# Row maxima turned by VectorE and carried to their rows by four small transfers per unit

## Chip, cores and metric

One core of one Trainium2 chip runs the program once. The metric is the device time of one execution in microseconds, the median of several runs. Everything computed is float32; the matmuls that matter here read float32r operands.

## What is computed

The reference is a transformer block over x of shape 8 x 512 x 512: attention with 16 heads of 32 (a latent of 128 for keys, values and queries, and a rotary part shared by the heads), then a shared feed-forward layer and 16 routed experts, each behind a layer norm and a residual. The part that the change touches is the softmax:

```python
k = jnp.concatenate([k_c, k_rb], axis=-1)
q = jnp.concatenate([q_c, q_rb], axis=-1)
scores = jnp.einsum('bhsd,bhtd->bhst', q, k) / math.sqrt(HEAD_DIM)
attn = jax.nn.softmax(scores, axis=-1)
ctx = jnp.einsum('bhst,bhtd->bhsd', attn, v_c)
```

The maximum over t of each row s is subtracted before the exponential. The kernel does that with an extra operand row of the scores matmul.

## The kernel before

All five engines run one long list of steps, `K.order`, and each engine takes from it the steps that it has a function for (the dictionaries `stages`). Attention is cut into 32 units `u`: eight batches (`b = u // 4`) of four groups of four heads (`g = u % 4`). `beside_order` (L170) lays 16 scores steps of unit u over 32 slots and puts the work of other stages between them, at slots given in the table `STEP` (L153): the maxima of the next unit (`tops`), the step `rows` that brings them to their place, the values, the keys and queries of unit u + 2 (`half`, then `send`), and a share of the work of the neighbouring batches.

The steps that bear on the change, for unit u, all of them but the scores done while unit u - 1 is at work:

- `top(u, j, i)`, 16 of them (j a head of the group, i a block of 128 query rows): TensorE makes the scores with the queries on the partitions (L632), VectorE takes the maximum of each row into `K.mx` (L925), a number per query row.
- `rows(u)`: TensorE turns the maxima of four heads by four small transposes (L638) into one of the two banks `MS`, so that they lie along four partitions, head by head. ScalarE writes them times -1 into the rows 64 to 67 of `K.QR[:, u % 2, :]` (L1433).
- `scores(u, i, j)`: TensorE makes the scores with the keys on the partitions, in two matmuls into one bank: 128 rows of content parts (L646), and 68 rows (L651), of which the rows 64 to 67 multiply the negated maxima with a constant (`c_sel`, one at the head's own row). The first L651 of a unit waits until `rows(u)` is done. ScalarE takes the exponential (L1443), GpSimd adds the blocks up for the sum (L1637).
- `send(u)`: SyncE issues eight transfers of 256 KB from SBUF to SBUF that stack the operands of unit u (L1792 to L1799); the first `top(u)` and the scores wait for them.

SyncE issues nearly all other transfers as well, on one queue, in the order of the list: loads of x (L1765), the second copy of a batch (`again`, L1808), `qr` (L1782, L1783: the shared rotary part of the queries into `K.QR`), the stores of x1 (L1813), of h (L1818) and of the turned h (L1824), 1 MB each. They come once per batch: the load of x and the store of h while the unit with g = 2 is at work, the store of the turned h in g = 3, `again` at the start of g = 0, the store of x1 in g = 1.

The banks `MS` are filled by turns, in the order in which the steps named in `FILLS` (L361) stand in the list; whoever fills one waits until the filling before the last was emptied.

## Time and profile before

| what | us |
|---|---|
| median of 3 runs (1570.11 to 1578.66) | 1576.51 |
| span of the profiled execution | 1566.3 |
| TensorE busy in it (matmuls) | 1498.5 |
| VectorE busy | 974.3 |
| GpSimd busy | 803.9 |
| ScalarE busy | 783.3 |
| DMA queue of SyncE, share of the 16 engines | 58.0% |

The span runs from the first to the last instruction of the program; the time of the profiled execution itself, with what lies around the span, is not given apart, so the runs' median stands in its place, 10.2 us above the span. A busy TensorE is not one at its peak, since its matmuls overlap. The attention part lies between about 60 and 860 us; the feed-forward part follows.

### The profile page before, as it was taken

What the parts mean: (1) busy time and instruction counts of PE and PEld (TensorE: products, weight loads), DVE (VectorE), ACT (ScalarE), POOL (GpSimd) and SP (SyncE); (2) the same over time, 40 slices, a digit from 0 to 9 for tenths busy, and PEclk for the clock granted to TensorE, in tenths of its full rate; (3) what the DMA queues carried; (4) which work ended last, traced back from release to release, by engine and by line L of the source; (5) the groups of instructions that cost most, each with busy time, mean ns of one, the idle gap of its engine ahead of it and who ended that gap; (6) DMA issues with size and microseconds to landing.
All of it is one profiled execution on the core that took longest, in us unless ns stands there. A gap on an engine that the chain in (4) does not pass through costs nothing.

```text
span 1566.3 us, 21725 instructions
## 1 busy us (share of the span) xinstructions
PE 1498.5 (96%) x7006; PEld 1018.5 (65%) x7006; DVE 974.3 (62%) x1841; ACT 783.3 (50%) x1415; POOL 803.9 (51%) x812
## 2 busy tenths in 40 slices
PE   5699999999999999999998999999999999999998
PEld 3355666656656666566564578778666666668886
DVE  3657676767676767767667454862333333349988
ACT  3265567566565675665647455422222222275554
POOL 1076787787776977877859630003222222143341
PEclk9699999999999999999999999999999999999999
DMA  5878669589495795884956421536987777697773
GB/s 130 138 100 135 101 109 213 74 173 172 82 179 111 121 211 74 181 156 85 222 97 129 135 79 67 198 121 196 311 235 219 210 215 221 195 349 241 232 241 125
DMA packets 163926, 257.75 MB, mean 165 GB/s; under 512 B 20100, under 2 KB 70404, under 8 KB 161764
## 3 DMA queue, kind: packets, MB, share of 16 engines
q1 hardware_dynamic: 144584, 204.98, 58.0%
q0 software_dynamic: 12784, 41.82, 9.4%
q10 hardware_dynamic: 6448, 9.57, 1.8%
q8 instruction: 58, 0.95, 0.3%
q14 instruction: 52, 0.43, 0.1%
HBM read 103.74 MB, written 58.46 MB: 104 GB/s over the span
## 4 chain that ended last, share of the span: by engine, by line
PE 71%; DMA 10%; DVE 7%; POOL 4%; issue 3%; ACT 2%; SPq 2%; DVEq 0%; POOLq 0%; ACTq 0%
PE bank L113 12%; PE bank L724 9%; PE bank L792 8%; PE bank L815 8%; PE bank L646 6%; PE bank L632 6%; DMA a<-a 6%; PE bank L662 6%; PE bank L651 6%; PE bank L746 5%; POOL a L1637 2%; PE bank L671 2%; DMA f<-f 1%; SPq L1875 1%; PE bank L804 1%
## 5 line engine op out<-in xcount | busy, mean ns | idle before, releaser
L1637 POOL TENSOR_TENSOR a<-a 128x512 f32<-128x512 f32 x384 | 499.5, 1329 | 100.2 <-ACT a L1443 54.5
L1443 ACT ACTIVATE a<-bank 128x512 f32<-128x512 f32 x512 | 296.4, 597 | 258.4 <-PE bank L651 218.4
L925 DVE TENSOR_REDUCE a<-bank 128x1 f32<-128x512 f32 x512 | 321.3, 680 | 80.2 <-PE bank L632 79.7
L113 PE MATMUL bank<-a 128*128 128x512 f32 (+1 forms) x864 | 238.9, 398 | 2.7 <-DVE s L877 1.6
L646 PE MATMUL bank<-a 128*128 128x512 f32 x512 | 217.3, 424 | 5.0 <-ACT a L1443 4.9
L651 PE MATMUL bank<-a 68*128 68x512 f32 x512 | 203.8, 398 | 0.4 <-ACT a L1433 0.2
L632 PE MATMUL bank<-a 128*128 128x512 f32 x512 | 181.0, 425 | 22.7 <-DMA a<-a 17.8
L113 PEld LDWEIGHTS bank<-a 128*128 128x128 f32 (+1 forms) x864 | 158.9, 186 | 49.1 <-issue 6.7
L1701 POOL DMA_INDIRECT f<-h_scratch,f x79 | 75.4, 954 | 224.5 <-DMA f<-f 203.6
L746 PE MATMUL bank<-c 128*128 128x512 f32 x768 | 178.2, 391 | 4.2 <-DVE c L983 2.1
L724 PE MATMUL bank<-c 128*128 128x512 f32 x768 | 177.4, 390 | 1.3 <-ACT c L1484 1.3
L746 PEld LDWEIGHTS bank<-c 128*128 128x128 f32 x768 | 143.6, 188 | 36.1 <-DVE c L983 3.4
L724 PEld LDWEIGHTS bank<-c 128*128 128x128 f32 x768 | 143.7, 188 | 34.5 <-issue 3.8
L646 PEld LDWEIGHTS bank<-a 128*128 128x128 f32 x512 | 96.8, 189 | 99.5 <-ACT a L1443 52.0
L792 PEld LDWEIGHTS bank<-f 128*128 128x128 f32 x632 | 119.7, 190 | 52.4 <-issue 40.1
L792 PE MATMUL bank<-f 128*128 x632 | 149.6, 380 | 2.3 <-issue 1.5
L815 PE MATMUL bank<-f 128*128 x316 | 148.5, 593 | 0.0
L632 PEld LDWEIGHTS bank<-a 128*128 128x128 f32 x512 | 96.7, 194 | 75.9 <-DVE a L925 28.6
L1258 DVE TENSOR_TENSOR f<-f 128x256 f32<-128x256 f32 x79 | 33.4, 423 | 173.4 <-ACT f L1556 173.3
L662 PE MATMUL bank<-a 128*32 128x512 f32 x1024 | 134.6, 612 | 0.0
L651 PEld LDWEIGHTS bank<-a 68*128 68x128 f32 x512 | 97.0, 189 | 16.0 <-ACT a L1433 1.2
L1566 ACT COPY f<-bank 128x512 f32<-128x512 f32 x79 | 46.3, 586 | 120.5 <-PE bank L815 118.1
(190 smaller groups left out, 1766.9 us busy)
## 6 DMA issues: line engine op xcount, KB each, us to landing
a<-a SPq DMA_DIRECT2D x272, 256.0 KB, 9.7
f<-f SPq DMA_DIRECT2D x316, 64.0 KB, 3.9
yp_scratch<-f SPq DMA_DIRECT2D x79, 256.0 KB, 3.4
a<-in_L_attn_x SPq DMA_DIRECT2D x15, 1024.0 KB, 11.7
x_scratch<-a SPq DMA_DIRECT2D x8, 1024.0 KB, 4.6
h_scratch<-a SPq DMA_DIRECT2D x8, 1024.0 KB, 13.3
hT_scratch<-s SPq DMA_DIRECT2D x8, 1024.0 KB, 9.8
c<-hT_scratch SPq DMA_DIRECT2D x8, 1024.0 KB, 7.0
```

The costliest lines, as they stand in the source:

```text
L113: t = e.matmul(out, a[n], b[n], start=n == 0 and m == 0, stop=n == len(ah) - 1 and m == 2)
L632: e.matmul(MX[n % 3][:], K.Qc[z][:, j, i * P:(i + 1) * P], K.Kc[z][:, j, :], start=True, stop=True).then_inc(Z.top, 1)
L646: e.matmul(SC[n % 2][:], K.Kc[z][:, j, i * P:(i + 1) * P], K.Qc[z][:, j, :], start=True, stop=False)
L651: e.matmul(SC[n % 2][:], K.KR[0:68, b % 2, j, i * P:(i + 1) * P], K.QR[0:68, u % 2, :], start=False, stop=True).then_inc(Z.score, 1)
L662: t = e.matmul(CT[HD * j:HD * j + HD, :], K.v[:, u % VS, i, HD * j:HD * j + HD], K.pt[:, n % NP, :], start=i == 0, stop=i == 3)
L724: t = e.matmul(bank[:], (K.sul if a else K.suh)[:, k, cut], (K.hTl if c else K.hTh)[:, k, :], start=m == 0, stop=m == 11)
L746: t = e.matmul(bank[:], (K.aTl if a else K.aTh)[:, k, cut], (K.sdl if c else K.sdh)[:, k, :], start=m == 0, stop=m == 23)
L792: t = e.matmul(K.UP[z][:, 0:FI], K.hTt[:, z, k * P:(k + 1) * P], K.flat[:, bass.ds(reg[i] + k * FI, FI)], start=k == 0, stop=k == 3)
L815: t = e.matmul(K.DN[z][:], K.eaT[:, z, k * P:(k + 1) * P], K.flat[:, bass.ds(reg[i] + 4 * FI + k * D, D)], start=k == 0, stop=k == 1)
L925: e.tensor_reduce(K.mx[:, i, j:j + 1], K.MX[n % 3][:], AX.X, ALU.max).then_inc(Z.max, 1)
L1443: e.activation(K.pt[:, n % NP, :], K.SC[n % 2][:], ACT.Exp, scale=SCALE).then_inc(Z.exp, 1)
L1637: e.tensor_tensor(K.acc[:, j, :], a, K.pt[:, n % NP, :], ALU.add).then_inc(Z.acc, 1)
```

## The change

The maxima now go into the columns 4j + i of a 128 x 32 tile `K.mx`, of which the other 16 columns are zero. `rows(u)` becomes a step of VectorE and of SyncE. VectorE turns the tile in its 32 x 32 blocks (one instruction) into `K.mxt`: partition 32a + 4j + i then holds the maxima of head j for the 32 query rows 128i + 32a and on. SyncE issues four transfers, one for each a, from 16 partitions of 128 bytes each into the rows 64 to 67 of `K.QR`. TensorE's four transposes and ScalarE's negation are gone, and so is this filling of `MS`, which shifts which of the two banks later steps use. The minus sign moves into the constant `c_sel`. The step `rows` is put at an earlier slot of the unit, right behind the last `top`.

```diff
@@ STEP: one of the four entries
-        "divide0": 1, "round0": 15, "low0": 15, "k0": 3, "q0": 5, "rows0": 25, "values0": (16, 16, 29),
+        "divide0": 1, "round0": 15, "low0": 15, "k0": 3, "q0": 5, "rows0": 23, "values0": (16, 16, 29),
...
-FILLS = ("turn", "proj", "half", "rows", "v", "total", "project", "turn2", "route", "fold", "bias")
+FILLS = ("turn", "proj", "half", "v", "total", "project", "turn2", "route", "fold", "bias")
...
-    K.mx = tile([P, 4, 4])
+    K.mx = tile([P, HD])
+    K.mxt = tile([P, HD])
@@ TensorE
-    def rows(u):
-        bank = begin("rows", u)
-        w.wait_ge(Z.max, 16 * (u + 1))
-        for i in range(4):
-            t = e.transpose(bank[0:4, i * P:(i + 1) * P], K.mx[:, i, :], K.ident[:])
-        t.then_inc(*end("rows", u))
...
         e.matmul(SC[n % 2][:], K.Kc[z][:, j, i * P:(i + 1) * P], K.Qc[z][:, j, :], start=True, stop=False)
-        drained("rows", u)
+        w.wait_ge(Z.shift, 4 * 16 * (u + 1))
@@ VectorE
+    e.memset(K.mx, 0.0).then_inc(Z.turned, 1)
...
         w.wait_ge(Z.top, n + 1)
+        w.wait_ge(Z.turned, u + 1)
+        e.tensor_reduce(K.mx[:, 4 * j + i:4 * j + i + 1], K.MX[n % 3][:], AX.X, ALU.max).then_inc(Z.max, 1)
+
+    def rows(u):
+        w.wait_ge(Z.max, 16 * (u + 1))
         if u:
-            m = K.fill["rows", u - 1]
-            w.wait_ge(Z.full[m % 2], m // 2 + 1)
-        e.tensor_reduce(K.mx[:, i, j:j + 1], K.MX[n % 3][:], AX.X, ALU.max).then_inc(Z.max, 1)
+            w.wait_ge(Z.shift, 4 * 16 * u)
+        e.transpose(K.mxt, K.mx).then_inc(Z.turned, 1)
@@ ScalarE
-    def rows(u):
-        b = u // NG
-        bank = begin("rows", u)
-        if u >= 2:
-            w.wait_ge(Z.score, 16 * (u - 1))
-        e.mul(K.QR[64:68, u % 2, :], bank[0:4, :], -1.0).then_inc(*end("rows", u))
@@ SyncE
+    def rows(u):
+        w.wait_ge(Z.turned, u + 2)
+        if u >= 2:
+            w.wait_ge(Z.score, 16 * (u - 1))
+        shift = raw(K.QR[64:68, u % 2, :]).rearrange("j (i s) -> j i s", s=P)
+        for a in range(4):
+            e.dma_start(shift[:, :, a * HD:(a + 1) * HD], K.mxt[a * HD:a * HD + 16, :]).then_inc(Z.shift, 16)
@@ constants
-        "c_sel": np.ascontiguousarray(np.broadcast_to(np.eye(4, dtype=np.float32)[:, :, None], (4, 4, S))),
+        "c_sel": np.ascontiguousarray(np.broadcast_to(-np.eye(4, dtype=np.float32)[:, :, None], (4, 4, S))),
```

The queue of SyncE from a unit with g = 2 into the next with g = 3. Before (L1799: last transfer of a send; L1775, L1776: rotary part of the keys; L1765: load of x; L1818: store of h; L1782, L1783: `qr`; L1792: next send):

```order
L1799 DMA a<-a 32x4x512
L1775 DMA a<-a 32x4x512
L1776 DMA a<-a 32x4x512
L1765 DMA a<-in_L_attn_x 128x4x512
L1818 DMA h_scratch<-a 128x4x512
L1782 DMA a<-a 32x512
L1783 DMA a<-a 32x512
L1792 DMA a<-a 32x4x512 x3
```

And now (the lines are those of the changed kernel: L1758 the load of x, L1819 the store of h, L1784 the four new transfers, L1775 and L1776 `qr`):

```order
L1800 DMA a<-a 32x4x512
L1768 DMA a<-a 32x4x512
L1769 DMA a<-a 32x4x512
L1758 DMA a<-in_L_attn_x 128x4x512
L1819 DMA h_scratch<-a 128x4x512
L1784 DMA a<-a 4x4x32 x4
L1775 DMA a<-a 32x512
L1776 DMA a<-a 32x512
L1793 DMA a<-a 32x4x512 x3
```

The four new transfers stand between the store of h and `qr`; the rest keeps its order.

The queue of VectorE at the same place, before (L925: maxima, L905: rotary part, L942: low part of the context):

```order
L905 TENSOR_TENSOR a<-a 64x512
L925 TENSOR_REDUCE a<-bank 128x1 x9
L942 TENSOR_TENSOR a<-s,a 128x512
L925 TENSOR_REDUCE a<-bank 128x1 x3
L912 SCALAR_TENSOR_TENSOR a<-bank,a 128x512
```

And now (L919: maxima, L925: the turn of the 32 x 32 blocks):

```order
L901 TENSOR_TENSOR a<-a 64x512
L919 TENSOR_REDUCE a<-bank 128x1 x9
L925 STREAM_TRANSPOSE a<-a 128x32
L942 TENSOR_TENSOR a<-s,a 128x512
L919 TENSOR_REDUCE a<-bank 128x1 x3
```

The turn comes right behind the last maximum of the unit, ahead of the low part of the context. On TensorE the four transposes L638 are taken out of the end of the unit, and no other matmul moves.

## Rows read from the trace of the kernel before

**Rows 1.** The page, head and part 1: busy us, share, instructions of each engine.

```profile
span 1566.3 us, 21725 instructions
...
PE 1498.5 (96%) x7006; PEld 1018.5 (65%) x7006; DVE 974.3 (62%) x1841; ACT 783.3 (50%) x1415; POOL 803.9 (51%) x812
```

**Rows 2.** Windows, one unit, columns: stretch, length, busy of PE, PEld, DVE, ACT, POOL, clock, DMA.

```profile
448.90:473.70 24.80, 24.80 (x143) 16.18 (x142) 16.25 (x31) 17.89 (x32) 18.50 (x21) 1.00 1.02 237
```

**Rows 3.** Timeline at the end of unit 14: start, length, engine, line, operation, idle before.

```profile
445.01 0.59 SPq L1818 DMA_DIRECT2D h_scratch<-a  x1
...
445.54 0.69 DVE L925 TENSOR_REDUCE a<-bank 128x1 f32<-128x512 f32 x1 [1.16 <-PE bank L632]
...
448.89 0.56 SPq L1782 DMA_DIRECT2D a<-a  x1
...
448.93 0.40 PE L651 MATMUL bank<-a 68*128 68x512 f32 x1
```

**Rows 4.** DMA view, issues of 445.01, 448.89, 449.50, 464.14, 517.03; last column us to landing.

```profile
h_scratch<-a SPq DMA_DIRECT2D x1, 1024.0 KB, 13.9
...
a<-a SPq DMA_DIRECT2D x1, 64.0 KB, 9.2
...
a<-a SPq DMA_DIRECT2D x1, 64.0 KB, 10.7
...
hT_scratch<-s SPq DMA_DIRECT2D x1, 1024.0 KB, 10.6
...
a<-a SPq DMA_DIRECT2D x1, 256.0 KB, 12.1
```

**Rows 5.** Chain of waits around 446.7 us: start, length, engine, line.

```profile
446.75 0.44 PE bank L638 x4
```

**Rows 6.** L1433 (ACT, negation), durations min/median/max in ns.

```profile
L1433 ACT ACTIVATE a<-bank x32: 585/586/588, 59.9 to 856.9; 4x512 fp32r<-4x512 f32 x32
```

**Rows 7.** VectorE, groups of 60 to 860 us.

```profile
L934 DVE RECIPROCAL a<-a 128x16 f32<-128x16 f32 x30 | 7.6, 254 | 1.0
```

**Rows 8.** The page, DMA issues, the smallest near an empty queue.

```profile
out<-c SPq DMA_DIRECT2D x1, 128.0 KB, 2.0
```

**Rows 9.** Line views of L1818, then of L1765: landing.

```profile
DMA to landing us min/median/max: 4.3/13.3/14.4
...
DMA to landing us min/median/max: 12.1/12.5/14.9
```

**Rows 10.** Timeline at other unit ends: last maximum, store or first score.

```profile
133.66 1.38 SPq L1765 DMA_DIRECT2D a<-in_L_attn_x  x1
...
139.32 0.39 PE L651 MATMUL bank<-a 68*128 68x512 f32 x1
...
473.75 0.40 PE L651 MATMUL bank<-a 68*128 68x512 f32 x1
...
492.34 0.69 DVE L925 TENSOR_REDUCE a<-bank 128x1 f32<-128x512 f32 x1 [0.48 <-PE bank L632]
...
502.30 0.40 PE L651 MATMUL bank<-a 68*128 68x512 f32 x1
...
529.16 0.40 PE L651 MATMUL bank<-a 68*128 68x512 f32 x1
...
854.86 0.67 DVE L925 TENSOR_REDUCE a<-bank 128x1 f32<-128x512 f32 x1
...
857.91 0.40 PE L651 MATMUL bank<-a 68*128 68x512 f32 x1
```

**Rows 11.** Windows around the first long stall.

```profile
43.80:48.20 4.40, 0.06 (x2) 0.01 (x1) 2.98 (x2) 1.90 (x1) 0.00 (x0) 0.81 1.05 187
61.30:69.90 8.60, 0.01 (x1) 0.00 (x0) 0.04 (x1) 0.60 (x1) 2.46 (x8) 0.50 0.85 118
69.90:73.80 3.90, 3.88 (x9) 3.11 (x10) 2.58 (x4) 1.30 (x2) 0.00 (x0) 0.50 0.00 0
73.90:78.00 4.10, 3.77 (x17) 2.76 (x16) 2.65 (x5) 3.12 (x6) 0.52 (x1) 1.00 0.29 62
```

More of the change, by code:

```diff
@@ L383, in __init__ @@
         self.top, self.max = make("top_full"), make("max_done")
+        self.turned, self.shift = make("mx_turned"), make("shift_in")
         self.score, self.exp, self.acc, self.pv = make("score_full"), make("exp_done"), make("acc_done"), make("pv_done")
@@ L817, in e_down @@
         t.then_inc(Z.ed, 1)
-    stages = {"turn": turn, "proj": proj, "v": v, "half": half, "bias": bias, "top": top, "rows": rows, "scores": scores,
+    stages = {"turn": turn, "proj": proj, "v": v, "half": half, "bias": bias, "top": top, "scores": scores,
               "values": values, "total": total, "project": project, "turn2": turn2, "route": route, "fold": fold, "up": up,
@@ L1342, in finish @@
         e.tensor_tensor(K.x1[:, z, :], K.x1[:, z, :], K.sh[:, z, :], ALU.add).then_inc(Z.co, 1)
-    stages = {"stat": stat, "aggr": aggr, "sel": sel, "split w": split_w, "turn": turn, "low": low, "proj": proj, "half": half, "bias": bias, "top": top, "invert": invert,
+    stages = {"stat": stat, "aggr": aggr, "sel": sel, "split w": split_w, "turn": turn, "low": low, "proj": proj, "half": half, "bias": bias, "top": top, "rows": rows, "invert": invert,
               "project": project, "fold": fold, "split h": split_h, "split up": split_up, "split down": split_down, "up": up,
@@ L1601, in finish @@
                      scale=K.crw[:, z, 4, 0:1]).then_inc(Z.cn, 1)
-    stages = {"split w": split_w, "round": round_, "scale": scale, "turn": turn, "proj": proj, "v": v, "half": half, "rows": rows, "scores": scores, "keep": keep,
+    stages = {"split w": split_w, "round": round_, "scale": scale, "turn": turn, "proj": proj, "v": v, "half": half, "scores": scores, "keep": keep,
               "turn2": turn2, "route": route, "split h": split_h, "split up": split_up, "round up": round_up,
@@ L1936, in finish @@
         e.dma_start(K.outv[t][:, cut], K.x1[:, z, cut]).then_inc(Z.cs[z], 16)
-    stages = {"load": load, "proj": proj, "qr": qr, "send": send, "again": again, "residual": residual, "scale": scale, "turn2": turn2, "early su": early_su,
+    stages = {"load": load, "proj": proj, "qr": qr, "rows": rows, "send": send, "again": again, "residual": residual, "scale": scale, "turn2": turn2, "early su": early_su,
               "early hT": early_hT, "load sd": load_sd, "split h": split_h, "weights": weights, "prepare": prepare, "move": move, "e down": e_down,
```

6 rows, old and new, of the table STEP are left out of this document.

## The prediction, made before the changed kernel ran

> **What bounds the kernel now.** I read the page first: TensorE is busy for 1498.5 us of the 1566.3 us span [rows 1]. The attention part (about 60 to 860 us, 32 units of work, four to a batch) was then cut into units with the windows view. In the unit that starts at 448.90 us TensorE is busy for all 24.80 us at the full granted clock, while VectorE, ScalarE and GpSimd have 16 to 19 us of work each, so anything that stops TensorE lengthens the kernel [rows 2]. The same row shows the DMA engines as full as TensorE (share 1.02). So the next view is the timeline at a unit's end [rows 3], to see how much time lies between the last row maximum of a unit (starts 445.54, ends 446.23) and the first scores matmul that needs the negated maxima (L651, 448.93): 2.70 us. And the DMA view tells what the sync queue holds at that moment [rows 3, 4]. A 1 MB store to h_scratch is issued at 445.01 and lands 13.9 us later, at 458.9. The two 64 KB transfers issued behind it, at 448.89 and 449.50, land after 9.2 and 10.7 us, at 458.1 and 460.2. They are small, yet they come out where the store does: **transfers of this queue leave it in the order in which they were issued.**
>
> **The change, part by part.**
> TensorE loses four 4x128 turns per unit, 0.44 us on the chain of waits [rows 5]. 32 units x 0.44 = 14.1 us, the whole gain that can be expected there. One filling of the two shared banks goes too; no wait of weight stands at it, so I cost it at nothing.
> ScalarE loses one negation per unit, 0.586 us x 32 = 18.8 us [rows 6]. It lies beside TensorE work; I take nothing for it. The minus sign moves into a constant and costs nothing.
> VectorE gains a turn of 128x32 per unit. The trace has no such shape; its nearest row is the 128x16 reciprocal with 0.25 us [rows 7], the lower bound is nothing. I take 0.2 us: 6 us in 32 units on an engine with a third of its time free. It counts only as part of the delay below.
> Sync gains four transfers of 2 KB per unit. Behind the waiting instruction on that queue stand, at most, the store of x1, the reload of x and the next unit's sends, which start over 5 us into a unit: no one waits for those. Who waits for the four is TensorE, at the first scores of a unit.
>
> So the cost is the landing of the four against that first matmul, which without the turns starts 0.44 us earlier. **The four have a time of their own**: turn and semaphores 0.3 us, three issues of 0.6 us before the last (0.56 us each for a 64 KB one [rows 3]), and 2.0 us to land, the fastest landing of the trace [rows 8]: about 4.2 us after the last maximum. And they have **the queue's time**: not before what was issued ahead of them, plus 0.3 us. The later one counts. Unit by unit (g is the unit's place in its batch):
>
> Into g=3, batches 1 to 6: the h store stands ahead. In the case of 448.93: 458.9 + 0.3 = 459.2 against 448.5, a wait of 10.7 us. The median store lands after 13.3 us instead of 13.9 [rows 9], so I take 10.1 us, times 6 = 61 us. In batch 0 the load of x stands there: issued 133.66, landing 12.1 us later at 145.8, plus 0.3, against 139.32 - 0.44: 7.2 us [rows 9, 10]. In batch 7 the store lands early, so the own time decides: last maximum 855.53 + 4.2 = 859.7 against 857.5, 2.2 us [rows 9, 10]. Sum 70 us.
> Into g=0 (seven): hT store, issued 464.14, lands 474.7, plus 0.3, against 473.75 - 0.44: 1.7 us [rows 4, 10]. But after the long wait the unit before starts on an empty queue, so this store should land some 0.6 us sooner in relation: 1.1 x 7 = 8 us.
> Into g=2 (eight): the sends of the next unit are ahead, the last issued 517.03, landing 529.1, plus 0.5, against 529.16 - 0.44: 0.9 x 8 = 7 us [rows 4, 10].
> Into g=1: last maximum 493.03 + 4.2 = 497.2 against 502.30 - 0.44: no wait [rows 10]. For the first two units, where TensorE already stood for transfers (8.60 us in a row with 0.01 busy), I add 1 us each [rows 11].
> Waits together: 70 + 8 + 7 + 2 = 87 us.
>
> **The clock.** After the 8.60 us without work the granted clock was 0.50 (1.2 GHz) and stayed there for the next 3.90 us of work, with 9 matmuls, against 17 in the 4.10 us after it at 1.00 (2.4 GHz); an idle stretch of 4.40 us already saw it fall (mean 0.81) [rows 11]. So 3.9 us at half rate lose about 1.9 us. The seven waits of 7 to 11 us each are long enough: 7 x 1.9 = 13 us. The Trainium skill (TensorE: Matmul & The Clock Gate, The HAM clock gate) says the same of an engine left idle; the trace agrees, and the sum uses the trace alone.
>
> Sum: 87 + 13 - 14 = +86 us. While TensorE stands, ScalarE and GpSimd work off what they are behind; TensorE's short waits for them are few, so I take 3 us back: **+83 us**. Against the profiled span that is 1566.3 + 83 = 1649.3 us. The span leaves out 10.2 us to the median of the runs shown (1576.5), in which the start and end around it lie; the profiled execution's own time isn't given apart. Forecast: 1576.5 + 83 = **1660 us**.
>
> **One rule of the skill against the rows.** The rows 3 and 4 show small transfers held by the store ahead. The Trainium skill (DMA: Bandwidth & Descriptors, Anatomy of one DMA) gives a transfer about 2.0 us fixed plus its bytes over a rate, that is some 2 us for 2 KB, with no word of what is ahead of it; by that price alone the sum would be that of the first rival. The same page (Queues, rings and completion order) has descriptors consumed in ring order on each engine, which the trace bears out, and splits a transfer over the largest number of rings, up to 16, that divides both outer sizes: 4 here, for 4 and 16. By that the four need only four of sixteen rings to be clear, which changes neither term as long as all rings are equally full.
>
> **The rivals.**
> 1. The small transfers pass what is queued, and only their own time counts (not slower). For it: they are tiny, and touch few of the engines. Against it: the two transfers behind the store [rows 3, 4]. Waits: into g=3 4.2 - 2.26 = 1.9 x 8 = 16 us, into g=0 0.4 x 7 = 3, start 1, less 14: +6 us. With issues of half that length (three of them 0.9 us less in all) it is -1 to -4. It decides where the four land within 2.3 us of the last maximum. Time: 1572 to 1583, say 1576; 7 in 100.
> 2. The order holds, but the waits are shorter: the store's data has left the rings some us before its write to memory is confirmed, or TensorE makes up time in the unit after. For it: the transfer of 448.89 lands 0.8 us before the store. Against: that is all of the difference, and the next one lands 1.3 us after. If a third of each long wait goes and no clock is lost in half of them: 83 - 23 - 7 = +53, 1630 us; 12 in 100.
> 3. The clock stays down for most of the unit after each long wait, since the unit begins with waits of its own. For it: nothing after 73.9 us. Against: 17 matmuls in 4.1 us at 1.00 right after the recovery. Its price goes to a unit of 24.80 us with 143 matmuls at half the rate, less what lies under waits: up to 15 us more x 7 = 105; half of that: +135, 1711 us; 4 in 100.
>
> **How the numbers follow.** My forecast's case has 77 in 100. Its own range comes from the long waits' landing (9.0 to 11.5 us each, +-9 us over seven), the short waits (8 to 25 us), the clock (0 to 25 us) and what is made up (0 to 15): 1635 to 1690. The range of 8 in 10 reaches into the second rival: 1622 to 1695. About 0.5% (8 us) is what a measurement of this kernel can tell from no change. Faster needs rival 1 with every saving: 0.02; within 0.5%: 0.05, the rest of rival 1; slower: 0.93.
>
> **What would show it.** In the changed profile TensorE should have gaps of 7 to 11 us before the first score's second matmul of seven units, spaced one batch apart, released by the small transfers, whose issue stands right after the h store and whose landing comes at or just after that store's. Each gap should be followed by some 4 us at a granted clock of 0.5. The units into g=1 should have no gap. The forecast is wrong if the four transfers land 2 to 3 us after issue while the store is still out, if the gaps are there but the next unit is shorter by as much, or if no gap shows and the span is near 1566 us.

## The result, and the profile after

| | us |
|---|---|
| before, median of 4 runs (1570.11 to 1578.66) | 1577.45 |
| changed, median of 4 runs (1664.62 to 1668.37) | 1666.47 |
| ratio, with its 95% interval | 1.0564 [1.0543, 1.0585] |

The changed kernel is slower by 89 us. The forecast was 1660 us, +83. The ratios here and below are over undisturbed runs; in e6, e7 and e12 they differ from the ratio of the two medians by 0.2 to 0.45%.

The head and part 1 of the changed kernel's page, then the line of its part 5 in which the difference stands:

```profile
span 1662.8 us, 21650 instructions
...
PE 1508.8 (91%) x6878; PEld 1025.6 (62%) x6878; DVE 979.5 (59%) x1874; ACT 769.4 (46%) x1383; POOL 801.2 (48%) x812
...
L646 PE MATMUL bank<-a 68*128 68x512 f32 x512 | 212.5, 415 | 92.4 <-DMA a<-a 92.4
```

TensorE was busy for 96% of the span [rows 1] and is now for 91%, with 128 fewer matmuls and yet 10 us more of busy time: part of its work ran at the lower clock, as the sums below show. One wait holds nearly all of the difference: the scores matmul with the maxima (L651 before, L646 now) stood for transfers for 92.4 us. Which transfers, the view of the one line that issues the four tells (count, time of one issue in ns, first and last start, then who waited):

```profile
L1784 SPq DMA_DIRECT2D a<-a x128: 625/632/713, 58.0 to 941.9; - x128
...
  PE bank L646: 92.4, 25
```

The timeline at the end of unit 14, the same place as [rows 3] (start, length, engine, line, operation; in brackets the idle time before it and who ended it), with the DMA view's landing time of the store ahead of the four; those of the 2 KB transfers are not recorded:

```profile
476.37 0.36 SPq L1819 DMA_DIRECT2D h_scratch<-a  x1
476.93 0.69 DVE L919 TENSOR_REDUCE a<-bank 128x1 f32<-128x512 f32 x1 [1.16 <-PE bank L634]
477.65 0.21 DVE L925 STREAM_TRANSPOSE a<-a 128x32 f32<-128x32 f32 x1
477.89 2.73 SPq L1784 DMA_DIRECT2D a<-a  x4
...
490.17 0.79 PE L646 MATMUL bank<-a 68*128 68x512 f32 x1 [10.18 <-DMA a<-a]
```

```profile
h_scratch<-a SPq DMA_DIRECT2D x1, 1024.0 KB, 13.0
```

The four are issued by 480.6, and the wait ends at 490.17. The store ahead of them, issued at 476.37, lands 13.0 us later, at 489.4. The matmul follows 0.8 us behind. The same row of other units (into g=3 of batch 0, into g=0 of batch 4, into g=3 of batch 6, and the last two units):

```profile
146.62 0.79 PE L646 MATMUL bank<-a 68*128 68x512 f32 x1 [7.53 <-DMA a<-a]
517.38 0.50 PE L646 MATMUL bank<-a 68*128 68x512 f32 x1 [0.32 <-DMA a<-a]
834.82 0.80 PE L646 MATMUL bank<-a 68*128 68x512 f32 x1 [7.75 <-DMA a<-a]
918.87 0.79 PE L646 MATMUL bank<-a 68*128 68x512 f32 x1 [3.09 <-DMA a<-a]
943.58 0.80 PE L646 MATMUL bank<-a 68*128 68x512 f32 x1 [3.18 <-DMA a<-a]
```

A matmul that begins a unit starts 0.23 us behind the one before it when nothing holds it. Measured against that (start less start, less 0.23), the 32 waits come to 97.4 us; the same sum is 1.7 us before. Into g=3: 7.7, then 10.4, 10.45, 10.3, 10.3, 10.5, 7.9 and, in batch 7, 3.4. Into g=0 0.45 to 1.5, into g=2 0.4 to 1.1 and once 3.25, into g=1 none but 0.3 in the first. The rest, 11.8 us (0.8 before), is the wait of the very first unit, which cost nothing: in the kernel before, TensorE stood for 8.60 us soon behind that place [rows 11], and the scores of unit 1 start at 92.7 us there and at 91.7 now.

The clock (windows view: stretch, length, busy time and count of PE, PEld, DVE, ACT, POOL, granted clock, DMA share and rate), in the wait of unit 15 and behind it:

```profile
480.30:490.17 9.87, 0.00 (x1) 0.01 (x1) 0.00 (x0) 0.09 (x1) 3.40 (x3) 0.73 0.93 284
490.20:495.10 4.90, 4.90 (x16) 4.14 (x17) 1.89 (x3) 2.04 (x4) 0.00 (x0) 0.50 0.00 0
495.10:499.10 4.00, 4.00 (x21) 2.19 (x20) 2.10 (x4) 2.81 (x5) 0.00 (x0) 0.99 0.00 1
```

It falls to 1.2 GHz while TensorE stands (a mean of 0.73 over the wait) and stays there for the first 4.9 us of work, in which 16 matmuls fit, against 21 in the 4.0 us behind it. It also falls where the wait was short. Two more windows, behind the wait of 1.1 us into g=0 that ends at 286.69 and behind that of 3.25 us that ends at 918.87:

```profile
286.90:290.30 3.40, 3.40 (x9) 2.65 (x9) 2.11 (x4) 1.19 (x2) 3.36 (x3) 0.50 0.89 304
...
918.80:925.20 6.40, 6.33 (x17) 4.33 (x21) 4.39 (x7) 2.68 (x5) 5.91 (x10) 0.50 0.92 315
```

**How far the attention part has moved.** The last scores matmul starts at 881.5 us before and at 967.4 now (first and last start are in each line's view):

```profile
L651 PE MATMUL bank<-a x512: 389/395/792, 60.5 to 881.5; 68*128 68x512 f32 x171
```

```profile
L646 PE MATMUL bank<-a x512: 389/395/797, 68.7 to 967.4; 68*128 68x512 f32 x171
```

So the part that the change touches is 85.9 us longer. From the scores of unit 1 on (92.7 before, 91.7 now) to that last start I took three sums from the trace: the length, the time in which no matmul runs, and the time in which one runs at a clock of 0.50, half of which is lost against full rate:

| | length | idle | at 0.50 | length - idle - half of that |
|---|---|---|---|---|
| before | 788.8 | 15.3 | 6.8 | 770.0 |
| changed | 875.7 | 92.0 | 54.1 | 756.6 |

The last column is TensorE's work at full rate, and 13.4 us less of it is left: the turns. In the twelve kernels below, which all do without the turns, it lies between 754.0 and 761.2 us, so the three columns account for their differences. Of the +86.9 us of length, 76.7 are idle, 23.6 the clock, and -13.4 the work.

The rest of the profiled span, which the change doesn't touch, is 10.6 us longer too (684.8 before, 695.4 now). TensorE stands in it for 25.5 us against 18.5, 6.2 us of that in one wait for ScalarE at 1504.8 us, and does 7.5 us of its work at a clock of 0.50 against none, which is worth 3.7. Over the fourteen profiles the rest lies between 684.8 and 698.9 us, shortest in the three in which TensorE does no work at 0.50 there. I compare kernels by their timed ratios, and the parts of a profile by the three sums.

### The profile page after: what moved, and what is told of

Its sections match the earlier page's. It is cut to its first block, busy times and chain, and to the rows that moved or that the text cites. A ratio compares the mean times of both kernels' runs of the same rounds, so it can differ in the third digit from the quotient of the medians.

```text
span 1662.8 us, 21650 instructions
## 1 busy us (share of the span) xinstructions
PE 1508.8 (91%) x6878; PEld 1025.6 (62%) x6878; DVE 979.5 (59%) x1874; ACT 769.4 (46%) x1383; POOL 801.2 (48%) x812
## 4 chain that ended last, share of the span: by engine, by line
PE 71%; DMA 9%; DVE 9%; SPq 3%; ACT 3%; issue 2%; POOL 2%; another core or an unknown queue 1%; DVEq 0%; POOLq 0%; ACTq 0%
PE bank L113 10%; PE bank L719 10%; PE bank L787 8%; DMA a<-a 8%; PE bank L810 8%; PE bank L741 7%; PE bank L634 6%; PE bank L646 6%; PE bank L641 5%; PE bank L657 5%; DVE a L919 4%; SPq L1784 3%; PE bank L666 2%; POOL a L1630 2%; PE bank L680 1%
## 5 line engine op out<-in xcount | busy, mean ns | idle before, releaser
L1630 POOL TENSOR_TENSOR a<-a 128x512 f32<-128x512 f32 x384 | 497.8, 1324 | 182.1 <-PE bank L666 124.9
L919 DVE TENSOR_REDUCE a<-bank 128x1 f32<-128x512 f32 x512 | 321.9, 681 | 159.6 <-PE bank L634 159.2
L646 PE MATMUL bank<-a 68*128 68x512 f32 x512 | 212.5, 415 | 92.4 <-DMA a<-a 92.4
L641 PE MATMUL bank<-a 128*128 128x512 f32 x512 | 220.5, 431 | 8.2 <-ACT a L1436 8.1
L634 PE MATMUL bank<-a 128*128 128x512 f32 x512 | 186.6, 437 | 8.3 <-DMA a<-a 4.5
L741 PE MATMUL bank<-c 128*128 128x512 f32 x768 | 180.1, 394 | 10.2 <-ACT c L1492 6.2
L646 PEld LDWEIGHTS bank<-a 68*128 68x128 f32 x512 | 100.3, 196 | 117.6 <-DMA a<-a 102.6
L641 PEld LDWEIGHTS bank<-a 128*128 128x128 f32 x512 | 99.1, 194 | 107.1 <-ACT a L1436 59.6
L634 PEld LDWEIGHTS bank<-a 128*128 128x128 f32 x512 | 101.4, 202 | 58.3 <-DVE a L919 27.6
```

The costliest lines, as they stand in the source:

```text
L634: e.matmul(MX[n % 3][:], K.Qc[z][:, j, i * P:(i + 1) * P], K.Kc[z][:, j, :], start=True, stop=True).then_inc(Z.top, 1)
L641: e.matmul(SC[n % 2][:], K.Kc[z][:, j, i * P:(i + 1) * P], K.Qc[z][:, j, :], start=True, stop=False)
L646: e.matmul(SC[n % 2][:], K.KR[0:68, b % 2, j, i * P:(i + 1) * P], K.QR[0:68, u % 2, :], start=False, stop=True).then_inc(Z.score, 1)
L741: t = e.matmul(bank[:], (K.aTl if a else K.aTh)[:, k, cut], (K.sdl if c else K.sdh)[:, k, :], start=m == 0, stop=m == 23)
L919: e.tensor_reduce(K.mx[:, 4 * j + i:4 * j + i + 1], K.MX[n % 3][:], AX.X, ALU.max).then_inc(Z.max, 1)
L1630: e.tensor_tensor(K.acc[:, j, :], a, K.pt[:, n % NP, :], ALU.add).then_inc(Z.acc, 1)
```

## The experiments

The theory was: the four transfers land when the queue ahead of them has landed; a wait of 10 us costs itself and a fall of the clock; and TensorE's turns are worth up to 14 us. The rivals: the four are slow in themselves, or the clock or the earlier slot of `rows` carries the loss. All expectations were written before the runs. Ratios are to the kernel before on the same chip; the last three columns are the profile's start of the last scores matmul, and TensorE's idle time and its work at 0.50 before it, as above (before: 881.5, 15.3, 6.8; changed: 967.4, 92.0, 54.1).

| run | edit to the changed kernel | us | ratio | last start | idle | at 0.50 |
|---|---|---|---|---|---|---|
| e1_store_behind | store of h behind the four | 1645.26 | 1.0431 [1.0398, 1.0464] | 956.5 | 75.4 | 63.6 |
| e2_both_behind | load of x behind them too | 1632.77 | 1.0359 [1.0324, 1.0394] | 935.7 | 59.3 | 52.9 |
| e3_act_queue | ScalarE issues the four | 1698.32 | 1.0766 [1.0730, 1.0802] | 1000.3 | 94.9 | 105.4 |
| e4_no_wait | nothing waits for the four | 1573.03 | 0.9975 [0.9961, 0.9989] | 876.1 | 20.9 | 12.4 |
| e5_all_vector | no transfer; turns and product on VectorE | 1576.41 | 0.9991 [0.9969, 1.0012] | 879.7 | 22.3 | 10.2 |
| e6_old_slots | `rows` at its slots of before | 1711.25 | 1.0874 [1.0833, 1.0914] | 1017.8 | 124.8 | 87.0 |
| e7_eight | eight transfers for four | 1720.54 | 1.0875 [1.0819, 1.0932] | 1020.6 | 124.9 | 91.0 |
| e8_one_turn | no transfer; one turn, four products | 1622.75 | 1.0335 [1.0318, 1.0351] | 936.2 | 55.0 | 59.4 |
| e9_act_no_wait | e4 with ScalarE issuing | 1653.73 | 1.0548 [1.0531, 1.0566] | 962.5 | 65.2 | 93.8 |
| e11_spread_late | wide turns, copy by ScalarE, old slots | 1608.07 | 1.0215 [1.0192, 1.0239] | 912.6 | 46.5 | 29.0 |
| e10_spread | the same, slots of the change | 1604.22 | 1.0184 [1.0151, 1.0217] | 907.1 | 37.4 | 36.6 |
| e12_spread_vector | the same, copy by VectorE | 1587.93 | 1.0076 [1.0045, 1.0106] | 913.6 | 43.0 | 35.8 |

One of the four runs of e7 took 6008.56 us, for a reason that I didn't find; the ratio leaves it out, and the other three took 1708.73 to 1721.28.

### What stands ahead in the queue (e1, e2)

```diff
@@ SyncE, e2; e1 holds back the store alone
+    held = []
     def load(b):
-        filled("proj", b - 1, "r")
-        e.dma_start(K.xt[:], x_d[b]).then_inc(Z.x, 16)
+        def fetch(): ...
+        if b > 1:
+            held.append(fetch)
+        else:
+            fetch()
...
             e.dma_start(shift[:, :, a * HD:(a + 1) * HD], K.mxt[a * HD:a * HD + 16, :]).then_inc(Z.shift, 16)
+        while held:
+            held.pop(0)()
...
         if i == 3 and kind == "h":
-            w.wait_ge(Z.scaled["h"], 4 * (b + 1))
-            e.dma_start(hv[b], K.yb[:]).then_inc(Z.h2s, 16)
+            def store(): ...
+            if b < B - 1:
+                held.append(store)
+            else:
+                store()
```

> The store of h is issued behind the four small transfers instead of ahead of them; nothing else moves. Theory (the transfers leave the sync queue in the order of issue): now the load of x is what stands ahead in batches 1 to 6. It landed 2.7 us before the store in the changed kernel (486.7 against 489.4), so the six waits into g=3 fall from 10.4 us to about 7.5, the clock still falls after them, and the time goes from 1666 to about 1648 (1643 to 1653). Rival (the small transfers are slow by themselves, as pieces of 128 bytes on four partitions, or the engines are full): the waits stay near 10 us and the time near 1666.

> The load of x and the store of h are both issued behind the four small transfers. Theory: what stands ahead is the rotary part of the keys, which landed at 484.2 against a first score at 479.8, so the waits into g=3 are some 4 to 5 us, in batch 0 too; 7 x 5.5 us less, and where the clock does not fall or comes back sooner up to 10 us more: 1618 to 1632, say 1626. Rival (slow by themselves): 1660 to 1670. A third outcome, that the late load of x holds up VectorE's next statistics, would show as waits of the maxima for the load of x and a time over 1640.

The timeline of e1 at the end of unit 14 (the store is L1824 here):

```profile
478.53 2.72 SPq L1786 DMA_DIRECT2D a<-a  x4
481.30 0.44 SPq L1824 DMA_DIRECT2D h_scratch<-a  x1
...
488.21 0.79 PE L646 MATMUL bank<-a 68*128 68x512 f32 x1 [7.56 <-DMA a<-a]
```

And of e2 (L1761 the load, L1829 the store):

```profile
468.95 2.71 SPq L1791 DMA_DIRECT2D a<-a  x4
471.70 0.44 SPq L1761 DMA_DIRECT2D a<-in_L_attn_x  x1
472.19 0.52 SPq L1829 DMA_DIRECT2D h_scratch<-a  x1
...
476.00 0.80 PE L646 MATMUL bank<-a 68*128 68x512 f32 x1 [4.93 <-DMA a<-a]
```

The waits into g=3 step down as the queue ahead is emptied: in batches 1 to 5, 10.3 to 10.5 us with load and store ahead, 7.7 to 8.0 with the load alone, 5.1 to 5.6 with neither. The time of e1 lies in what was expected; e2 missed by a little (waits of 4 to 5 us and 1618 to 1632 us expected, 1632.77 measured). The transfers are the same four, so they aren't slow in themselves; **what is ahead of them is**. At this place the matmul goes 0.7 to 0.8 us behind the landing of the last transfer ahead each time: of the store (489.4 and 490.17), in e1 of the load (487.46 and 488.21), in e2 of the rotary part of the keys (475.21 and 476.00). The idle time falls with them, 92.0, 75.4, 59.3 us. The clock gives nothing back (54.1, 63.6, 52.9 us at 0.50): it falls behind a wait of 5 us as behind one of 10.

### Another engine's queue (e3, e9)

```diff
@@ ScalarE, e3 and e9; rows is taken from SyncE
+    def rows(u):
+        w.wait_ge(Z.turned, u + 2)
...
+        for a in range(4):
+            e.dma_start(shift[:, :, a * HD:(a + 1) * HD], K.mxt[a * HD:a * HD + 16, :]).then_inc(Z.shift, 16)
```

> The same four transfers, issued by ScalarE on its own queue, with the wait for VectorE's turn on ScalarE. Theory (queue order): they pass the sync queue, and only their own time counts, 4 to 5 us after the last maximum: waits into g=3 of 2 to 3 us, the others near 0, 15 to 25 us in all instead of 97, and no fall of the clock. Against it stands ScalarE's time at four issues (some 0.63 us each, 2.5 us a unit in which no exponential runs), which TensorE feels in part: up to 60 us. Together 1580 to 1625, say 1600. Rival (the 16 engines are what is full, whatever the queue): the waits stay at 8 to 10 us and the time is over 1650.

This missed by far, and was the most telling run. The waits into g=3 of batches 0 to 6 fell to 3.9 to 4.8 us, yet the time rose. ScalarE at the end of unit 14, with the store of h that SyncE issued at 496.12, and TensorE (the order in the fence is SyncE, ScalarE, TensorE):

```profile
496.12 0.72 SPq L1819 DMA_DIRECT2D h_scratch<-a  x1
...
497.62 2.64 ACTq L1434 DMA_DIRECT2D a<-a  x4
500.31 1.09 ACT L1444 ACTIVATE a<-bank 128x512 f32<-128x512 f32 x2 [3.24 <-issue]
...
500.96 0.80 PE L641 MATMUL bank<-a 128*128 128x512 f32 x1 [2.10 <-ACT a L1444]
...
506.08 0.80 PE L646 MATMUL bank<-a 68*128 68x512 f32 x1 [3.47 <-DMA a<-a]
```

Two things stand in it. On their own queue the four do pass the store: it lands at 508.7 (12.6 us), and the matmul goes at 506.08. But their last one, issued at 499.62, still took about 6.5 us, not 2.0. Over these 6.5 us the sixteen DMA engines had a share of 1.06 (windows view), so they were full of the other queue's work. In the changed kernel, into the last unit, the same step took 1.7 us (last issue 941.86, matmul 943.58) with that share at 0.02. The Trainium skill (DMA: Bandwidth & Descriptors, Issuing engines are not separate DMA queues) says that transfers of different issuers run on the same engines and interleave, which these numbers bear out. And ScalarE pays: four issues of 0.64 to 0.66 us, in which its next exponential stands for 3.24 us and TensorE behind it for 2.10.

That page of the Trainium skill adds that another issuer saves only the time to initiate a transfer, "usually small relative to the DMA itself". To weigh this time alone I took the waiting away and left the issuing, on SyncE (e4) and on ScalarE (e9):

```diff
@@ e4, e9: TensorE waits for the zeroed rows only; the four go to rows nobody reads
-        w.wait_ge(Z.shift, 4 * 16 * (u + 1))
+        w.wait_ge(Z.rope0, 1)
...
-        shift = raw(K.QR[64:68, u % 2, :]).rearrange("j (i s) -> j i s", s=P)
+        shift = raw(K.QR[96:100, u % 2, :]).rearrange("j (i s) -> j i s", s=P)
```

> Leaves out the subtraction of the row maxima: the four transfers are issued as in the changed kernel, but into rows that nobody reads, TensorE does not wait for them, and the rows 64 to 67 hold zero. Everything else (maxima, turn, issues, slots) is as in the changed kernel. Theory: the whole loss is TensorE's wait for the landing and the clock after it, so the kernel ends up below the one before by the four turns of TensorE: 1577 - 14 = 1563, between 1558 and 1570. Rival (a share of the loss lies in the transfers or their issue, which delay the sends behind them, or in the other order of the banks): 1575 to 1600.

> The version without the wait (maxima not subtracted, transfers into rows that nobody reads), with the four transfers issued by ScalarE instead of SyncE. If ScalarE's time at the issues is what made the version on ScalarE's queue slow, its loss shows here without any wait for a landing: the first score of a unit came 2.6 us later after the last maximum there, 32 x 2.6 = 83 us on top of 1573, so 1640 to 1665. Rival (that version was slow through the landings alone): 1573 to 1585.

The waits of TensorE in e9, from 60 to 960 us (waited for: us in total, times, longest):

```profile
PE bank L642 <- ACT a L1446: 53.7, 42, 4.1
```

The issues cost nothing on SyncE (e4 is at 0.9975) and 5.5% on ScalarE, as much as 32 x 2.64 us, 84 us, of issuing, although ScalarE is busy for only half of the span. By the sums it comes in two parts: against e4 TensorE stands for 44 us more (65.2 against 20.9) and works 81 us more at the low clock (93.8 against 12.4), which is worth 41. The unit's exponentials come one by one and hand TensorE's two score banks back, so a hole of 2.6 us among them isn't hidden, and many of these stops (the clock falls 22 times between the second unit and the end of the attention part) are followed by a stretch at half rate. "Small relative to the DMA itself" is true here of 0.64 us against 6.5, and says nothing of the engine that issues.

e4 also prices the term of the sum that was taken for sure. It should have been 14 us faster than before, and was 4 (0.25%); its last start is 5.4 us earlier. The work at full rate is 12.4 us less (757.6 against 770.0), so the turns are gone nearly in full, but TensorE stands for 5.6 us more (in this stretch it waits for the sends for 7.9 us against 4.8, and for ScalarE for 7.0 against 4.3) and works 5.6 us more at 0.50. Part of a saving on the busiest engine turns into waits for the next slowest.

### The slot of rows (e6)

```diff
-"rows0": 23, ... "rows1": 21, ... "rows2": 25, ... "rows3": 25,
+"rows0": 25, ... "rows1": 26, ... "rows2": 28, ... "rows3": 28,
```

> The change with the step rows at the slots that it had before (25, 26, 28, 28 instead of 23, 21, 25, 25). Theory (the later of the own time and the queue's time decides): into g=3 the queue decides, so those waits stay at 10.4 us; into g=0 and g=2 the own time takes over, since the turn comes 2 to 3 us later, and those waits grow from about 0.9 and 0.5 us to about 2.5 and 1.1; into g=1 there is still room. Together some 17 us more: 1675 to 1690, say 1683. Rival (all waits are the queue's): 1666, as the change.

The timeline of e6 into a unit with g=2, and what the DMA view has for the store of x1 (L1814):

```profile
472.99 0.75 DVE L880 SCALAR_TENSOR_TENSOR a<-bank,a 128x512 fp32r<-128x512 f32 x1 [2.89 <-ACT a L1406]
473.65 0.20 DVE L925 STREAM_TRANSPOSE a<-a 128x32 f32<-128x32 f32 x1
...
475.28 0.36 SPq L1814 DMA_DIRECT2D x_scratch<-a  x1
475.69 3.37 SPq L1784 DMA_DIRECT2D a<-a  x4
...
480.25 0.79 PE L646 MATMUL bank<-a 68*128 68x512 f32 x1 [4.18 <-DMA a<-a]
```

```profile
x_scratch<-a SPq DMA_DIRECT2D x1, 1024.0 KB, 4.3
```

The waits into g=3 of batches 1 to 5 are as they were (10.3 to 10.6 us), as expected, since the same store is ahead either way. The miss is elsewhere: into g=2 of batches 1 to 6 the waits are 4.2 to 4.8 us, not 1.1, and those of batch 7 are 7.1 us into g=2 and 8.5 into g=3. The last maximum ended at 470.09, and the four are issued from 475.69. Of these 5.6 us 3.6 are VectorE's: its turn has come behind a step that waits for ScalarE, and starts at 473.65. Another 1.4 us are SyncE's: at slot 26 the four have come behind the store of x1 (slot 23), and SyncE waits for that store's data until 475.28. The idle time grows by 32.8 us, and the clock takes half of another 32.9. So the earlier slots are part of what keeps the change at +89 and not +134 (by the medians): what an order of steps costs includes **what stands ahead on each engine of the path, and what that waits for**.

### The number of transfers (e7)

> Twice the transfers: four of the same shape into rows that nobody reads are issued ahead of the four that count. Theory (own time against queue time): the last issue comes 2.8 us later, 7.9 us after the last maximum. Waits into g=3 in batches 0 to 6, where the queue decides, stay as they are within 0.5 us (10.4); into g=0 they go from 0.9 to about 4 us, into g=2 from 0.5 to about 2, into g=1 they stay at 0; about 40 us in all: 1695 to 1715, say 1706. Rival (each of these transfers of 128-byte pieces costs time on the rings): the waits into g=3 grow by 1 us or more as well, and the time is over 1720.

The edit puts four dead transfers of the same kind ahead of the four. The waits into g=3 grow by 0.8 us only (11.0 to 11.35 in batches 1 to 5), for four issues of 0.63 are 2.5 us and lie under the store's landing. That is between the 0.5 us of the theory and the 1 us of the rival; what the 0.8 us are was not tested. Those into g=0, where now the own time decides, grow from 0.5 to 1.5 us to 2.9 to 4.2. The windows view behind such a wait (the one that ends at 548.74):

```profile
548.70:553.00 4.30, 4.26 (x10) 3.39 (x11) 2.58 (x4) 1.19 (x2) 1.66 (x2) 0.50 0.73 244
```

10 matmuls in 4.3 us at 0.50, behind a wait of 3 us. The waits come to 133 us against 97 (about +40 was expected), the idle time to +32.9 us, and the work at 0.50 to +36.9, half of which, 18 us, is what the expectation had too little of.

### Without transfers (e5, e8)

```diff
@@ VectorE, e5
-        e.transpose(K.mxt, K.mx).then_inc(Z.turned, 1)
+        for a in range(4):
+            e.transpose(K.mxt[64:96, a * HD:(a + 1) * HD], K.mx[a * HD:(a + 1) * HD, :]).then_inc(Z.turned, 1)
+        w.wait_ge(Z.turned, 4 * u + 5)
...
+        e.tensor_tensor(K.QR[64:80, u % 2, :].rearrange("r (i s) -> r i s", s=P),
+                        K.mxt[64:80, :].unsqueeze(1).broadcast_to([16, 4, P]),
+                        K.mask[64:80, :].unsqueeze(2).broadcast_to([16, 4, P]), ALU.mult).then_inc(Z.shift, 1)
@@ VectorE, e8: the one turn stays, and four products, one from each quarter of the partitions
+            e.tensor_tensor(K.QR[64:80, u % 2, :].rearrange("r (i s) -> r i s", s=P)[:, :, at.start:at.start + HD],
+                            K.mxt[at, :].unsqueeze(1).broadcast_to([16, 4, HD]),
+                            K.mask[at, :].unsqueeze(2).broadcast_to([16, 4, HD]), ALU.mult).then_inc(Z.shift, 1)
```

VectorE's turn can write to other partitions than it reads, so four turns of 32 x 32 bring the maxima next to their rows. A product with a mask of minus ones keeps from each of 16 rows the part that is its own. The matmul then has 80 rows for 68, at the same 395 ns.

> A version without transfers: VectorE turns the maxima in four blocks of 32x32 straight into partitions 64 to 95, which gives 16 rows of 128 (one per head and block of rows), and one VectorE product with a mask of minus ones and zeros spreads them over 512 columns of the operand's rows 64 to 79; the constant has 16 rows and the second scores matmul reads 80 rows instead of 68. No turn on TensorE, no negation on ScalarE, no filling of a shared bank, no wait for a landing. Theory (the loss is the landing alone, and what can be had without it is what the kernel without the wait showed): no wait of the first score, about 1.3 us of VectorE work a unit in its place, 1570 to 1577, a hair below the kernel before. Rival (VectorE's extra 1.3 us a unit hold up the maxima, 32 x 1.3 = 42 us on an engine that TensorE waits for at the ends of units): 1585 to 1615.

> As the all-VectorE version, with less work in it: one turn of 128x32 in place of four of 32x32 (0.20 us each there), and four products of 16 partitions x 128 elements, which also shift the rows to partitions 64 to 79, in place of one of 512 elements (1.34 us there). Theory: the last product is done about 1.4 us after the last maximum instead of 2.2, so the 0.3 us that TensorE still waited into g=3 goes, and the kernel comes near the one without a carry (1573): 1571 to 1576. Rival (the four products cost as much as the one, each being held by something fixed): 1576 to 1580.

e5's turns and its product in the view of their lines (min/median/max in ns), and the one wait for it:

```profile
L927 DVE STREAM_TRANSPOSE a<-a x128: 202/203/208, 57.6 to 855.0; 32x32 f32<-32x32 f32 x128
```

```profile
L932 DVE TENSOR_TENSOR a<-a x32: 682/1382/1823, 58.5 to 855.3; 16x512 fp32r<-16x512 f32 x32
```

```profile
PE bank L647 <- DVE a L932: 3.8, 9, 2.2
```

e5 runs level with the kernel before and is the best version that computes everything. It shows that the loss lies in the transfers: the same maxima, turned by the same engine, cost nothing without them. e8 was to show the same with fewer instructions, and lost 3.4%. The view of its product, and its VectorE timeline at one place, with GpSimd's at the same time:

```profile
L933 DVE TENSOR_TENSOR a<-a x128: 282/1239/9861, 59.2 to 911.7; 16x128 fp32r<-16x128 f32 x128
```

```profile
549.07 10.81 DVE L933 TENSOR_TENSOR a<-a 16x128 fp32r<-16x128 f32 x4
```

```profile
548.89 1.29 POOL L1674 TENSOR_TENSOR a<-a 128x512 f32<-128x512 f32 x1
550.13 2.53 POOL L1640 TENSOR_TENSOR a<-a 128x512 f32<-128x512 f32 x2
552.62 1.28 POOL L1674 TENSOR_TENSOR a<-a 128x512 f32<-128x512 f32 x1
553.85 4.94 POOL L1640 TENSOR_TENSOR a<-a 128x512 f32<-128x512 f32 x4
```

Four products that take 0.28 us each at best last 10.81 us, 9.86 of them in the first, as long as GpSimd works without a pause. TensorE waited 34.4 us for them in all, and the clock fell with it. In e5 VectorE's product met such a row of GpSimd instructions too, and was through after 1.82 us, while GpSimd went on:

```profile
264.15 6.70 POOL L1639 TENSOR_TENSOR a<-a 128x512 f32<-128x512 f32 x5
264.16 1.82 DVE L932 TENSOR_TENSOR a<-a 16x512 fp32r<-16x512 f32 x1
```

### Which instructions wait for GpSimd (e11, e10, e12)

If products with two inputs are what waits, a kernel without any on this path should not. I put the maxima of block i into a tile of their own, so that four turns of 32 x 128 leave every row complete; one copy to `K.QR` is left, by ScalarE (times -1) or by VectorE (the sign in `c_sel`):

```diff
-    K.mx = tile([P, HD])
+    K.mx = tile([P, 4, HD])
...
+        spread = K.stage.rearrange("r (i s) -> r i s", s=P)
+        for a in range(4):
+            e.transpose(spread[:, :, a * HD:(a + 1) * HD], K.mx[a * HD:(a + 1) * HD, :, :]).then_inc(Z.turned, 1)
@@ ScalarE, e10 and e11; in e12 VectorE: e.tensor_copy(K.QR[64:80, u % 2, :], K.stage[0:16, :])
+        e.mul(K.QR[64:80, u % 2, :], K.stage[0:16, :], -1.0).then_inc(Z.shift, 1)
```

> A version without transfers and without VectorE products. The maxima are written into a tile of 128 x 4 x 32 that is zero but for column 4j + i in block i, so that four turns of VectorE (32 partitions x 128) give the 16 rows already spread over 512 columns; ScalarE copies them, times -1, into the operand (16 partitions x 512, as long as the negation before, 0.59 us). The step stands at the slots of the kernel before (25, 26, 28, 28). No TensorE turn, no shared bank. Theory (what the small products cost in the last version was a wait for GpSimd, which instructions with one input do not have): the turns take 0.2 to 0.35 us each whatever GpSimd does, no wait of TensorE of weight at the first score, ratio to before 0.995 to 1.000. Rival (VectorE's four more instructions or ScalarE's wait for them hold up TensorE): ratio over 1.003.

> The same with the step at the slots of the change (23, 21, 25, 25), right behind the last maximum. ScalarE then waits for the last maximum and the four turns, up to 2 us a unit in which no exponential runs. If waiting ScalarE is what delays TensorE (part of what made the version on ScalarE's queue slow), this one is slower than the other by 10 to 40 us; if only the issue of transfers on ScalarE was to blame there, both are equal within 4 us.

> As the last two, with the copy into the operand made by VectorE (one input, 16 x 512, 0.65 us by the nearest shape) instead of ScalarE, at the slots of the change, the minus sign in the constant. If ScalarE's waiting for VectorE was what cost those versions 2%, it is gone here: the operand is ready about 4 x 0.30 + 0.65 = 1.95 us after the last maximum, in time for every first score but perhaps 0.1 us into g=3; ratio to before 0.994 to 1.000. Rival (the turns on VectorE themselves hold up TensorE): ratio 1.01 or more.

The copy by ScalarE in e11 (part of the line view: busy us, mean ns, idle before it and whom it waited for), then the turns and the copy of e12:

```profile
L1434 ACT ACTIVATE a<-a 16x512 fp32r<-16x512 f32 x31 | 19.4, 626 | 41.4 <-DVE a L927 41.3
```

```profile
L927 DVE STREAM_TRANSPOSE a<-a x128: 302/303/307, 59.4 to 889.2; 32x128 f32<-32x128 f32 x128
```

```profile
L931 DVE CAST a<-a x32: 417/1038/8953, 60.8 to 889.6; 16x512 fp32r<-16x512 f32 x32
```

The turns never wait for GpSimd (302 to 307 ns in 128 of them), and VectorE's copy does, five times for 8.9 to 8.95 us, each time until 0.3 us after GpSimd's row of instructions ended, though it has one input. My guess of the two inputs was too narrow, and e11 and e12 missed. e10 and e11 lose to something else: ScalarE stands for the turns for 41.3 us in e11 and 49.8 in e10, and TensorE waits for its exponentials for 28.4 and 29.6 us, against 4.9 before and 8.0 in e12, where ScalarE has no part in the step. e10 was expected to lose 10 to 40 us against e11 if ScalarE's waiting were to blame. It was 4 us faster; but ScalarE waits for the turns in both, so the pair can't tell, and it is the comparison with e12 that speaks for the waiting. That e10 with the earlier slots is no slower also shows that the slot is not the reason. The runs of e12 scatter (1570.87 to 1600.59 us) and its profile is one of the longest (span 1598.8), so I take the durations from it; by its ratio it is 0.8% slower than the kernel before.

## Why the prediction was right, and where its terms were off

The forecast was +83 us, the measured difference is +89, and in the profiles the attention part grew by 85.9. By terms, in us:

| term | forecast | measured |
|---|---|---|
| waits into g=3, eight | 70 | 71.1 |
| into g=0, seven | 8 | 5.8 |
| into g=2, eight | 7 | 7.4 |
| into g=1, start of the part | 2 | -0.8 (0.3 less 1.1) |
| made up (less idle elsewhere) | -3 | -7.9 |
| clock | 13 | 23.6 |
| TensorE's turns | -14.1 | -13.4 |

The misses partly cancel (the clock took 10.6 us more, 4.9 more were made up, and the waits besides those into g=3 were 4.6 less), so that the total is nearer than its terms is in part luck.

- **The queue's time** was right. The waits into g=3 of batches 1 to 5 were 10.3 to 10.5 us against 10.1, batch 0's 7.7 against 7.2, and e1 and e2 show the cause by moving it. There the matmul went 0.7 to 0.8 us behind the store's landing, where 0.3 stood. Two entries inside were off and partly cancel: batch 6, whose store landed after 11.5 us and not 13, waited 7.9 us (and its matmul went 0.1 us before that landing, so the order isn't exact), and batch 7 3.4 where 2.2 stood. Those into g=2 were 0.4 to 1.1 us in seven of eight, and one, at the end of the attention part, 3.25. Into g=0 the store of the turned h decided, as forecast: it landed at 517.21, and the matmul went at 517.38.
- **The own time** of 4.2 us took the landing of 2.0 us from an empty queue [rows 8]. That was right where the engines were idle: 1.7 us from the last issue to the matmul into g=3 of batch 7, and 1.7 into g=0 of e7 (547.01 and 548.74). The issues were 0.67 to 0.73 us apart (0.6 taken), the turn took 0.21 us (0.2 taken). Under load the landing is longer: 6.5 us in e3, where no store was ahead on its own queue. What batch 7 waited above the forecast is the turn, which the forecast had right behind the last maximum. It stood behind a product of the feed-forward part and began 1.7 us late:

```profile
937.86 1.83 DVE L979 TENSOR_TENSOR c<-f,c 128x512 fp32r<-128x512 f32 x1
939.62 0.20 DVE L925 STREAM_TRANSPOSE a<-a 128x32 f32<-128x32 f32 x1
```

- **The clock** is the term that was mis-sized, 13 us for 23.6. Behind the seven long waits it was low for 3.1 to 6.0 us of work (32 us together, or 16 lost; the forecast had 3.9 each, from [rows 11]). The other 22 us lie in five stretches that the forecast didn't have, since it let only waits of 7 us and more bring the clock down: behind waits of 1.1, 1.4, 3.25 and 3.4 us, and one near the end, behind a stop of 2.1 us. Before there were two, each with 3.4 us of work, behind stops of 1.9 and 2.0 us; the second is at that same place near the end.
- **The turns** went nearly in full, 13.4 us of 14.1. As a gain in time they are worth less: in e4, where no wait for the four hides it, 4 us were left, since other waits and the clock took the rest.
- **ScalarE's and VectorE's terms** at nothing hold as far as e4 tells: it has both and is no slower than the kernel before. The same engines are not free for everything, though: issuing on ScalarE (e9) cost its full time.
- **The 10.2 us** between span and median were put down to what lies around the span. That was wrong: a run's time is 1.8 us above its span (1664.62 against 1662.8), and 1.8 or 1.9 us in all 64 runs of the kernel before that were timed beside the experiments. The profiled execution before was a fast one, at about 1568 us below all four runs of the first table. The clock is a part of that: its mean was 0.988 in the profile, 0.986 to 0.989 in those of the 64 with a span up to 1567.4 us, and 0.981 to 0.985 in those with 1575.0 and more. A difference of 0.003 over 1570 us is 4.7 us, by my estimate about half of what lies between them. What starts the fall stays open; no run was made for it.
- **The rivals.** That small transfers pass is refuted on the same queue (e1, e2) and true across queues (e3), where it doesn't help. The price of some 2 us that the prediction takes from the Trainium skill (DMA: Bandwidth & Descriptors, Anatomy of one DMA) is fitted there to transfers that GpSimd issues; here SyncE's took 1.7 us with the DMA engines idle, and what is queued comes on top. Shorter waits: not seen. The clock staying down for most of a unit: not seen, at most 6.0 us of work behind a long wait (and 21 matmuls in 4.0 us right behind 495.1), though right in that the clock would cost more than 13 us.

No version here that computes everything beats the kernel before; e5 equals it.

## What to carry to other kernels

A small transfer costs what is queued ahead of it, not its bytes: before putting one on a path with little slack (2.7 us here), add up what the queue holds at that moment and what its issuer still waits for. If the path is TensorE's, count the fall of the clock too, behind short waits as well: in these kernels each us of added idle time brought 0.3 to 0.9 us more (e4 and e5 aside, where both are small). Moving the issue to a compute engine's queue trades this for that engine's time, 2.64 us for four here, which a half-idle engine can't hide when it feeds TensorE one tile at a time. The sums of idle time, half of the work at low clock and the rest split any such difference into its causes.

## What the runs showed of the hardware, unexpected

- VectorE can be held across several instructions of GpSimd: up to 9.9 us for one 16x128 product (0.28 at best), up to 8.95 us for one 16x512 copy (0.42 at best), while the turns kept their time within 6 ns. The Trainium skill (SBUF — State Buffer, SBUF: two separate sides) has an exclusive lock between the two engines, held "for the whole instruction", against which VectorE's two-input work and its faster modes compete. That it is exclusive agrees; that the loser stands through eight instructions of the other in a row (548.89 to 558.79) is more than it says. It isn't always so: the product of e5, also with two inputs, took at most 1.8 us, though GpSimd's instructions followed each other as closely there. Why stays open.
- Transfers on ScalarE's queue passed a 1 MB store on SyncE's that was issued 1.5 us ahead, and still needed 6.5 us for 2 KB with the DMA engines full (share 1.06). With a share of 0.02 the same took 1.7 us.
- TensorE's clock fell to 1.2 GHz around waits of only 1.1 to 3.4 us, and was low for 3.4 to 6.4 us of the work behind them; most other waits of about 1 us had no fall. What makes the difference stays open.
- The matmul with 80 rows for 68 took the same time (medians 395 and 395 ns).
